# Pairs of an attention phase placed by the width of its slots, the first half's projection later, and the gate products on GpSimd

## The reference, cut to what matters

```
mod = (silu(c) @ wmod)                      # per image: sa, ca, ga, sb, cb, gb
h = layernorm(x) * (1 + ca) + sa
q = [heads(q_c @ W_qdec), rope(heads(q_c @ W_qrope))]      # q_c = h @ W_q
k = [heads(kv_c @ W_kdec), rope(heads(h @ W_krope))]       # kv_c = rms(h @ W_kv) * g_kv
x = x + ga * (softmax(causal(q @ k.T * scale)) @ v @ W_o)
h = layernorm(x) * (1 + cb) + sb
t = (h @ Wm + bm) in 8 groups of 32
w, i = top2(softmax(t @ expert_emb))
x = x + gb * (sum_k w_k * (gelu(t @ W1[i_k] + b1) @ W2[i_k] + b2) @ Wo + bo)
```

## Time and profile before

| | |
|---|---|
| median of 3 runs | 3072.03 us (3066.36 to 3072.98) |
| profiled execution | 3070.06 us, span 3068.3 us |
| mean granted TensorE clock | 0.970 |
| TensorE busy | 2880.1 us, 94% of the span |
| VectorE, ScalarE, GpSimd busy | 62%, 59%, 43% |
| opening until the first slot of image 0 | 98 us |
| attention phase, images 1 to 7 | 172.6 to 175.7 us each |
| expert phase, images 0 to 6 | 195.0 to 196.6 us each |

### The profile page before, as it was taken

How to read it: one execution, slowest core, us unless ns; L and a number is a source line. 1 busy time by engine, 2 the same in 40 slices (tenths; PEclk the granted TensorE clock), 3 DMA queues, 4 the chain that set the end, 5 groups by cost and what they waited for, 6 DMA issues and landing times.

```text
span 3068.3 us, 51536 instructions
## 1 busy us (share of the span) xinstructions
PE 2880.1 (94%) x16460; PEld 1276.4 (42%) x16460; DVE 1908.1 (62%) x4637; ACT 1804.0 (59%) x2146; POOL 1320.1 (43%) x1355
## 2 busy tenths in 40 slices
PE   5689999999998999999999999999999999998999
PEld 2243444444444444444444444444444444444433
DVE  5465766757657566665666656665656747657453
ACT  1145665556754667546674466654766556754686
POOL 3312465225552364514644246532465225552254
PEclk8699999999999999999999999999999999999999
DMA  5201453024530344204442054310453123530242
GB/s 137 43 25 32 120 137 87 26 59 114 135 91 1 94 110 128 67 1 108 118 109 65 7 128 122 102 41 25 124 135 87 29 57 103 138 87 16 67 127 90
DMA packets 176245, 252.54 MB, mean 82 GB/s; under 512 B 50797, under 2 KB 82557, under 8 KB 175885
## 3 DMA queue, kind: packets, MB, share of 16 engines
q1 hardware_dynamic: 168988, 247.26, 31.2%
q10 hardware_dynamic: 6996, 1.99, 0.3%
HBM read 159.13 MB, written 12.63 MB: 56 GB/s over the span
## 4 chain that ended last, share of the span: by engine, by line
PE 85%; DVE 6%; issue 3%; ACT 1%; POOL 0%; SPq 0%; DMA 0%; POOLq 0%; ACTq 0%; DVEq 0%
PE ps L1248 18%; PE ps L1211 17%; PE ps L1266 16%; PE ps L1232 9%; PE ps L412 8%; PE ps L458 4%; PE ps L510 2%; PE ps L529 2%; PE ps L499 2%; PE ps L460 2%; DVE front L555 2%; PE ps L486 1%; PE ps L517 1%; PE ps L444 1%; PE ps L468 1%
## 5 line engine op out<-in xcount | busy, mean ns | idle before, releaser
L1332 ACT ACTIVATE rest<-ps 128x1024 f32<-128x1024 f32 x1024 | 992.8, 1022 | 370.5 <-PE ps L1248 368.7
L1314 ACT ACTIVATE rest<-ps 128x1024 f32<-128x1024 f32 (+3 forms) x768 | 608.3, 810 | 649.9 <-PE ps L1211 638.5
L1419 POOL TENSOR_TENSOR rest<-rest 128x512 f32<-128x512 f32 x480 | 630.0, 1313 | 650.5 <-DVE rest L1368 644.0
L1248 PE MATMUL ps<-wide,w1s 98*128 98x512 f32 x2048 | 623.8, 425 | 11.3 <-ACT rest L1332 8.5
L552 DVE CUSTOM_DVE_ANT_0 rest<-ps,maskd 128x128 f32<-128x128 f32 (+3 forms) x1024 | 460.7, 488 | 223.4 <-PE ps L412 215.4
L1409 POOL TENSOR_SCALAR_AFFINE_SELECT rest<-rest 128x256 f32<-128x256 f32 x512 | 211.0, 420 | 888.3 <-ACT rest L1314 885.2
L1266 PE MATMUL ps<-rest,w2s 128*32 128x512 f32 x4096 | 547.1, 606 | 0.6 <-ACT rest L1332 0.6
L1248 PEld LDWEIGHTS ps<-wide,w1s 98*128 98x128 f32 x2048 | 339.7, 188 | 492.6 <-ACT rest L1332 354.9
L1368 DVE SCALAR_TENSOR_TENSOR rest<-ps,b2c,wide 128x512 f32<-128x512 f32 x512 | 382.5, 747 | 260.1 <-PE ps L1266 233.6
L1211 PE MATMUL ps<-wide 49*128 49x512 f32 (+3 forms) x2304 | 500.7, 523 | 5.4 <-ACT rest L1314 4.9
L555 DVE TENSOR_REDUCE front<-ps 128x1 f32<-128x512 f32 x512 | 329.6, 685 | 211.7 <-PE ps L412 207.2
(11 more groups left out here) (136 smaller groups left out, 2292.0 us busy)
## 6 DMA issues: line engine op xcount, KB each, us to landing
wide<-gate_rows SPq DMA_DIRECT2D x1024, 128.0 KB, 2.8
wide<-front SPq DMA_DIRECT2D x480, 64.0 KB, 2.0
wide<-front SPq DMA_DIRECT2D x192, 128.0 KB, 2.3
ao<-in_x SPq DMA_DIRECT2D x16, 512.0 KB, 5.1
heads<-front SPq DMA_DIRECT2D x64, 128.0 KB, 2.4
xs<-in_x SPq DMA_DIRECT2D x16, 512.0 KB, 4.9
out<-xs SPq DMA_DIRECT2D x16, 512.0 KB, 3.4
wide<-ao SPq DMA_DIRECT2D x96, 64.0 KB, 2.3
```

What stands on the lines that cost most here:

```text
L1248: mm = pe.matmul(bank(2 * (u % 2) + k), L.w1s[:, e, :], L.x2[:, c, 4 * j + 2 * p + k, :], start=True, stop=True)
L1314: nc.scalar.activation(L.pt[:, u % PTS, :, f:HALF], L.ps[:, 2 * (u % 2):2 * (u % 2) + 2, 0:HALF - f], ACT.Exp, scale=SCALE).then_inc(S["c_ ...
L1332: nc.scalar.activation(L.hm[:, u % HM, :], bank(2 * (u % 2), 2), ACT.Gelu).then_inc(S["e_gelu"], 1)
L1419: g.tensor_tensor(dst, dst, L.gy[:, k % GY, :], ALU.add).then_inc(S["e_add"], 1)
```

## The change

1. Images 1 to 7 take the pairs of an attention phase by the table `PLACES`, one entry per pair with its slot and its list (0 between, 1 behind). Before, slots 9 to 36 had two pairs each and the slots 0, 2 to 8 one. Now 60 pairs stand in 36 slots: slots 18, 19, 22, 23, 30, 31 have one, slots 4 and 8 two, slot 6 none.
2. Four pairs of group 1's second half (`AHEAD`) are computed at the end of the expert phase of the image before. For that the pairs there start earlier: the second half of group 0 in steps 36 to 51 (was 38 to 53), group 1's first half in 52 to 59 (was 55 to 62), the four new ones in 60 to 63, the row of group 1 in 62 (was 63).
3. In all images the projection of the first half is later: `tr` one slot, `o` four, `xn` and `stats` three and four, `tr2` to `lg` two; the chain's links 3 to 17 stand three to a slot from slot 40 (two to a slot from 37). `gt` stays in slot 45.
4. The gate products go from VectorE (behind slot 22) to GpSimd (behind slot 20).

```diff
+AHEAD = 4
+PLACES = [(0, 1), (1, 0), (2, 0), (3, 0), (4, 0), (4, 1), (5, 0), (7, 0), (8, 0), (8, 1)]
+PLACES += [(s, part) for s in range(9, 15) for part in range(2)] + [(15, 0), (15, 1)]
...
     if img:
-        pairs = [(s, ("pair", 1, *p)) for s, p in zip((0, 2, 3, 4, 5, 6, 7, 8), PAIRS[1])]
...
+        places = PLACES
+        pairs = [("pair", 1, *p) for p in PAIRS[1][AHEAD:AHEAD + 10]]
+        pairs += [("pair", g, *p) for g in (2, 3) for p in PAIRS[0]]
+        pairs += [("pair", 1, *p) for p in PAIRS[1][AHEAD + 10:]]
+        pairs += [("pair", g, *p) for g in (2, 3) for p in PAIRS[1]]
...
+    ropes = {s: ("rope", 8 + k) for k, s in enumerate((0, 2, 3, 4, 5, 6, 7, 8))}
+    for (s, part), pair in zip(places, pairs):
+        if img == 0 and slots[s][0]:
+            part = 1
+        if part and img and s and s in ropes:
+            slots[s][1].append(ropes.pop(s))
+        slots[s][part].append(pair)
+    for s, rope in ropes.items():
+        slots[s][1].append(rope)
...
-    slots[26][1].append(("tr", 0, 0))
-    slots[27][1].append(("tr", 0, 1))
-    slots[28][1].append(("o", 0, 0))
-    slots[29][1].extend([("o", 0, 1), ("stats", 0)])
-    slots[31][1].append(("xn", 0))
-    slots[33][1].extend([("tr2", 0, 0), ("tr2", 0, 1)])
...
+    slots[27][1].append(("tr", 0, 0))
+    slots[28][1].append(("tr", 0, 1))
+    slots[32][1].append(("o", 0, 0))
+    slots[33][1].extend([("o", 0, 1), ("stats", 0)])
+    slots[34][1].append(("xn", 0))
+    slots[35][1].extend([("tr2", 0, 0), ("tr2", 0, 1)])
...
     for k in range(3, 18):
-        slots[37 + (k - 3) // 2][1].append(("chain", 0, k))
+        slots[40 + (k - 3) // 3][1].append(("chain", 0, k))
...
     for k, p in enumerate(PAIRS[0]):
         at(28 + k, ("pair", 0, *p))
-        at(55 + k, ("pair", 1, *p))
+        at(52 + k, ("pair", 1, *p))
     for k, p in enumerate(PAIRS[1]):
-        at(38 + k, ("pair", 0, *p))
+        at(36 + k, ("pair", 0, *p))
+    for k, p in enumerate(PAIRS[1][:AHEAD]):
+        at(60 + k, ("pair", 1, *p))
     at(36, ("row", 0, 0))
     at(54, ("row", 0, 1))
-    at(63, ("row", 1, 0))
+    at(62, ("row", 1, 0))
...
-                    if s == 22:
-                        v.wait_ge(S["a_mod"], 96)
...
+                    if s == 20:
+                        g.wait_ge(S["a_mod"], 96)
+                        if img:
+                            RA[img].wait(g, L, ("out", 3))
+                        for k in range(CH):
+                            g.tensor_tensor(L.wog[:, k, :], L.wos[:, k, :], L.gate[:, 0, :],
+                                            ALU.mult).then_inc(S["d0_w"], 1)
...
```

More of the change, by code:

```diff
@@ L1048 @@
 NQ = NU // 2
+AHEAD = 4
+PLACES = [(0, 1), (1, 0), (2, 0), (3, 0), (4, 0), (4, 1), (5, 0), (7, 0), (8, 0), (8, 1)]
+PLACES += [(s, part) for s in range(9, 15) for part in range(2)] + [(15, 0), (15, 1)]
+PLACES += [(16, 0), (16, 1), (17, 0), (17, 1), (18, 0), (19, 0), (20, 0), (20, 1), (21, 0), (21, 1), (22, 0), (23, 0)]
+PLACES += [(s, part) for s in range(24, 30) for part in range(2)] + [(30, 0), (31, 0)]
+PLACES += [(s, part) for s in range(32, 37) for part in range(2)]
 def attend_slots(img):
@@ L1056, in attend_slots @@
         slots[1][1].extend([("out", 2), ("out", 3)])
-    if img:
-        pairs = [(s, ("pair", 1, *p)) for s, p in zip((0, 2, 3, 4, 5, 6, 7, 8), PAIRS[1])]
-        pairs += [(9 + k // 2, ("pair", 2, *p)) for k, p in enumerate(PAIRS[0])]
-        pairs += [(13 + k // 2, ("pair", 3, *p)) for k, p in enumerate(PAIRS[0])]
-        pairs += [(17 + k // 2, ("pair", 1, *p)) for k, p in enumerate(PAIRS[1][8:])]
-    else:
-        pairs = [(k * 7 // 16, ("pair", 0, *p)) for k, p in enumerate(PAIRS[1])]
-        pairs += [(9 + k // 3, ("pair", 2, *p)) for k, p in enumerate(PAIRS[0])]
-        pairs += [(12 + k // 3, ("pair", 3, *p)) for k, p in enumerate(PAIRS[0])]
-        pairs += [(15 + k * 6 // 16, ("pair", 1, *p)) for k, p in enumerate(PAIRS[1])]
+        places = PLACES
@@ new lines, in attend_slots @@
+        pairs = [("pair", 1, *p) for p in PAIRS[1][AHEAD:AHEAD + 10]]
+        pairs += [("pair", g, *p) for g in (2, 3) for p in PAIRS[0]]
+        pairs += [("pair", 1, *p) for p in PAIRS[1][AHEAD + 10:]]
+        pairs += [("pair", g, *p) for g in (2, 3) for p in PAIRS[1]]
+    else:
+        places = [(k * 7 // 16, 0) for k in range(16)] + [(9 + k // 3, 0) for k in range(8)]
+        places += [(12 + k // 3, 0) for k in range(8)] + [(15 + k * 6 // 16, 0) for k in range(16)]
+        places += [(21 + k // 2, 0) for k in range(32)]
+        pairs = [("pair", 0, *p) for p in PAIRS[1]] + [("pair", g, *p) for g in (2, 3) for p in PAIRS[0]]
+        pairs += [("pair", g, *p) for g in (1, 2, 3) for p in PAIRS[1]]
@@ L1067, in attend_slots @@
         slots[7][0].append(("rmax", 0))
         slots[7][1].append(("row", 0, 1))
-    pairs += [(21 + k // 2, ("pair", 2, *p)) for k, p in enumerate(PAIRS[1])]
-    pairs += [(29 + k // 2, ("pair", 3, *p)) for k, p in enumerate(PAIRS[1])]
-    for s, pair in pairs:
-        slots[s][1 if s == 0 or slots[s][0] else 0].append(pair)
-    for k, s in enumerate((0, 2, 3, 4, 5, 6, 7, 8)):
-        slots[s][1].append(("rope", 8 + k))
+    assert len(places) == len(pairs)
+    ropes = {s: ("rope", 8 + k) for k, s in enumerate((0, 2, 3, 4, 5, 6, 7, 8))}
@@ L1377, in _ @@
                         item_vector(v, L, RA[img], item)
-                    if s == 22:
-                        v.wait_ge(S["a_mod"], 96)
-                        for k in range(CH):
-                            v.tensor_tensor(L.wog[:, k, :], L.wos[:, k, :], L.gate[:, 0, :],
-                                            ALU.mult).then_inc(S["d0_w"], 1)
-                            v.tensor_tensor(L.wfg[:, k, :], L.wfs[:, k, :], L.gate[:, 1, :],
-                                            ALU.mult).then_inc(S["d0_w"], 1)
-                        v.tensor_tensor(L.bog[:, :], L.bor[:, :], L.gate[:, 1, :], ALU.mult).then_inc(S["d0_w"], 1)
                 for q in range(NQ):
@@ L1431, in _ @@
                         L.clear(g, L.names_b)
+                    if s == 20:
[5 more added lines that the diff above has]
+                                            ALU.mult).then_inc(S["d0_w"], 1)
+                            g.tensor_tensor(L.wfg[:, k, :], L.wfs[:, k, :], L.gate[:, 1, :],
+                                            ALU.mult).then_inc(S["d0_w"], 1)
+                        g.tensor_tensor(L.bog[:, :], L.bor[:, :], L.gate[:, 1, :], ALU.mult).then_inc(S["d0_w"], 1)
                     if s == 33:
```

8 lines of the change are left out of this document (4 added, 4 removed).

## The result

The changed kernel takes 3038.09 us (median of 6 runs, 3035.65 to 3051.42) against 3067.02 us of the kernel before beside it (6 runs, 3064.14 to 3072.98): ratio 0.9914, 95% interval 0.9893 to 0.9934. In a second comparison the ratio was 0.9904 (0.9884 to 0.9923). The profiled execution took 3048.61 us, span 3046.9 us, mean granted clock 0.974.

A forecast was written before the change was run, and what follows sets the result against it. TensorE, busy 94% of the span, was taken as the bound. 7 x (8.9 - 7.9) - 5.2 = +1.8 us on the profiled 3070.06 gave 3071.9, or 3074 as a median; range 3050 to 3102.

The forecast's parts named there:

- gaps, attention: TensorE's waits in attention, images 1 to 7: six narrow-slot gaps go, the normalisation's shrinks, small waits come; -4.4 us an image.
- clock, attention: Stretches at half clock in attention nearly all go: 0.5 us of 4.0 kept, -3.5 us an image.
- TensorE's own work, both phases: Net cost of moving four pairs' work from attention to the experts: between 0 and 1.0 us, taken as 0.4.
- gaps, experts: Steps q 36, 37, 54 and 62: items wait for readers of the two-bank ring; +5.7 us a phase.
- clock, experts: New expert gaps bring 1.7 stretches at half clock per phase: +2.8 us, bounds none and 6.6.
- so only three things can change: With TensorE's work unchanged, only gaps in attention, gaps among the experts and stretches at the lower clock could differ.
- The rival that the clock is kept: The experts' new gaps, each under 1.7 us, don't lower the clock: 3054 us, chance 0.26.
- the one that it falls twice in each phase: Gaps at q 36 and 37 and at q 54 each bring two low-clock stretches every phase: 3101 us, chance 0.24.
- Its premise on the memset: Slots 32 to 36: GpSimd's memset starts 3 us before the normalisation and ends before that is half through; gaps 1.7 us.
- new wait for the row of maxima: Shorter attention slots leave less time for the row's DMAs: 0.4 us of waits at slots 20, 24 and 32.
- Image 0: It keeps its pairs but has the later projection: gaps -0.22 - 0.98 - 1.4, clock -2.6, together -5.2 us.
- rival of GpSimd being late: Gate products at 1.31 us delay slot 21's masks; `values` waits 1.5 us in 8 images: 3086 us, chance 0.06.

The follow-up runs named there:

- memset behind the normalisation: The kernel before, with GpSimd's memset of slot 33 waiting for the normalisation instead of the statistics: 3029.6 us, ratio 0.9882.
- first trace: The changed kernel with all its parts against the kernel before, first comparison: 3038.1 us, ratio 0.9914; its profiled execution took 3048.61 us.
- pairs alone: The changed kernel with projection and gate products put back as in the kernel before: 3080.2 us, ratio 1.0035.
- second trace: The changed kernel once more, unaltered, against the kernel before: 3039.4 us, ratio 0.9904.
- projection alone: The kernel before with only the first half's projection and its chain later, pairs and gate products as before: 3019.9 us, ratio 0.9839.

## Why the prediction was wrong

The mechanisms that it named were all met, but one that it ruled out was at work beside them. The sizes were off, all in the same direction, and the sum is then multiplied by seven. Terms per image, in us; the measured work is TensorE's busy time in windows rows without a low stretch, so that neither gap nor clock is in it; the clock is what is left of the difference in length. No attention phase of the kernel before is without a low stretch, so its work is that of the run with the memset behind the normalisation, where TensorE has the same order.

| term | predicted | measured |
|---|---|---|
| gaps, attention | -4.4 | -4.65 (10.27 to 5.62) |
| clock, attention | -3.5 | -3.6 in the first trace, -3.4 in the second |
| TensorE's own work, both phases | +0.4 | -0.9 |
| gaps, experts | +5.7 | +4.9 (4.5 to 9.4) |
| clock, experts | +2.8 | +2.0 in the first trace, +1.1 in the second |
| sum | +1.0 | -2.4 (first trace), -2.9 (second) |

- **The step that failed first** is the sentence that TensorE's work is the same before and after, "so only three things can change". TensorE's busy time for the same matmuls at the full clock depends on what they stand beside and wait for. With before's order on TensorE it is 159.53 us a phase (memset behind the normalisation), with the projection later 158.76, with the pairs placed by width 158.11, and with four pairs gone 156.51. The last step, -1.6, comes back among the experts as +2.1 (190.81 to 192.91, the undisturbed phase of the pairs alone): that net of +0.5 is the term that the prediction had, at 0.4. The other 1.4 us an image, ten for the kernel, had no term at all. With -0.9 for +0.4 this is the largest miss in the sum, 1.3 of the 3.4 us an image in the first trace.
- **Gaps among the experts:** 0.88 + 0.74 at q 36 (predicted 0.9 + 0.9), 1.57 at q 37 (1.64), 0.88 + 0.49 at q 54 (0.9 + 0.75), 0.39 at q 62 (0.6). Each wait was named with its reader, and all was right but the size: a row waits only for what is left of a pair's read, and the reads of narrow pairs are short (at q 54 VectorE reads a bank of 256 columns in 0.42 us, one of 512 takes 0.69). The prediction's lower bound of 4.7 is 4.8 by its own working (5.7 less six times 0.15), and its upper one of 7 had none; the sum came out near the lower. That the phase grew by 8.9, as predicted, is luck: 2.1 of it is the work that was put at 0.4 (the prediction took that as a net of both phases), and gaps and clock are smaller by as much.
- **Clock among the experts:** taken as 1.7 stretches for each phase. Behind the new gaps stood 23.9 us of low clock in seven phases in the first trace and 13.6 in the second: one stretch of 3.4 a phase, or 0.6. The rival that the clock is kept was half right, the one that it falls twice in each phase wrong. The stretches can't be counted from the gaps: phases of one order had none (202.1), one (203.7) or two (205.2).
- **Attention:** the six small gaps went, 3.45 us, as predicted. The normalisation's gaps were put at 1.7 and are 0.84 + 0.90 in the profiled image, so the hand-made order of slots 32 to 36 held. Its premise on the memset did not: it begins 1.43 us ahead of the normalisation, not 3, so that 2.1 of its 3.51 us are met, and it ends when the normalisation (3.20 us) is past its half, not before. That the sum is right all the same is in part luck. The 0.5 us of clock kept back was not needed. The new wait for the row of maxima (0.4) was 1.48 in the pairs alone; in the changed kernel no image of the trace has one over 0.2.
- **Image 0** was forecast at -5.2: -5.9 in the second trace, +0.2 in the first, which had the long low stretch. **The last expert phase** (-3.1 and -1.9) had no term; its low stretches were 15.0 us before and 3.4 and 8.1 after, and it differs as much between kernels that are alike there (176.2 and 172.4).
- **The gate products** were put at nothing, which the run confirms; the product measured 0.72 where 0.65 was estimated. The rival of GpSimd being late is out.
- **The range** took each term's bounds as if they would offset each other. They are the same steps in seven images, so an error of 3.4 to 3.9 us an image is 24 to 27 us. Its lower end would have had to be seven times the lower bounds of all terms together.

What the parts are worth was not asked in the prediction, and this is what the runs show best. By its own terms the later projection is worth 15 us (its gap and image 0) without the clock and 40 with all of it, and the experts cost 62. Measured, the projection brings 50 alone, the gate products 0, and the pairs cost 10 alone and some 20 on top of the projection. Within the pairs, the places by width gain 16 (3020 to 3004, one comparison) and the four pairs sent ahead cost 34 (3004 to 3038, across two). So two parts gain 66 us, and a third gives half of it back.

Open stays why equal orders differ in their low stretches from image to image. Why TensorE's busy time shrinks by 0.8 us when only the projection's items move is open too, but the traces say where. Taken from each matmul's start to the next one's, less the idle time shown, the scores and pairs of slot 32 take 2.60 us with the gap of 0.98 among them (memset behind the normalisation) and 2.33 without it (projection alone), those of slot 38 1.33 and 1.06; the two slots are 0.54 of the 0.77. The record of a 512-wide score matmul lasts 0.59 us, and the next may start 0.31 to 0.43 us after it began. So busy time is not work alone: some of a wait can stand under the end of the matmul before it, and a gap that goes can be worth more than its idle time. How much of the term is that, and how much is work, no run here takes apart.

## What to carry to other kernels

Where a gap of the bounding engine stands behind another engine's block, look at what runs beside that block on the engine that can hold it up: here one changed wait, so that a GpSimd memset starts behind VectorE's normalisation, was worth more than a table of sixty places. Price moved work at both ends from undisturbed rows, and ask separately what the work left behind costs in its new neighbourhood. Split a change before you judge it: an item sent to a phase where the bounding engine has no gap beside it pays its whole wait there. Here four pairs relieved attention by 2.9 us an image, cost the experts 8.7, and the kernel lost 34 us.
